# Cross-attention and ternary FFN on one core: A's scale from norms, prologue work spread over eight steps, row maxima in PSUM, a new block order, and the FFN two steps earlier

## The reference

```python
h = layernorm(x)                                   # (16, 128, 256)
q = rmsnorm(heads(h @ Wq)) * gq                    # over each head's 128
k = rmsnorm(heads(ctx @ Wk)) * gk
v = heads(ctx @ Wv)
x = x + concat(softmax(q @ k.T / sqrt(128)) @ v) @ Wo
h = layernorm(x)
# bit_linear: activations rounded to 8 bits per row, weights to -1, 0, 1 by their mean |w|
h = silu(bit_linear(h, w_gate)) * bit_linear(h, w_up)
x = x + bit_linear(rms_norm(h) * ln_weight, w_down)
```

## Time and profile before

| | before |
|---|---|
| median of 3 runs | 529.06 us |
| profiled execution: time, span | 530.74 us, 528.90 us |
| mean granted TensorE clock | 0.974 of full |
| busy share TensorE, VectorE, ScalarE, GpSimd | 80%, 92%, 81%, 73% |
| first 27.2 us | loads, maxima, scales |
| 27.2 to 107.9 us | steps 0 to 7 |
| 107.9 to 413.8 us | 56 steps |
| 413.8 to 442.1 us | attention's tail, first FFN steps |
| from 442.1 us | FFN |

### The profile page before, as it was taken

The page is one execution under the profiler, slowest core; times in us unless marked ns, Lnnn a source line. Parts: engine busy times, 40 slices in busy tenths (PEclk is TensorE's granted clock), DMA queues, the critical chain, the costliest instruction groups (busy, mean ns, idle before and its releaser), DMA issues.

```text
span 528.9 us, 14416 instructions
## 1 busy us (share of the span) xinstructions
PE 420.7 (80%) x4456; PEld 316.9 (60%) x4456; DVE 484.6 (92%) x1303; ACT 428.1 (81%) x1447; POOL 386.8 (73%) x312
## 2 busy tenths in 40 slices
PE   0248275699999999999999999999999556678885
PEld 0137264577777777677776777777777343345554
DVE  1989969899999999999999999999999857899995
ACT  1079488498988989889898898988989638799983
POOL 1015628479989899998989999899989943666772
PEclk9999877799999999999999999999999999899999
DMA  7950713154734445354444535445464530000001
GB/s 278 347 170 22 233 46 81 41 81 85 155 79 100 99 91 108 79 114 85 99 99 84 114 79 111 87 95 104 89 114 85 117 60 2 1 20 32 30 30 51
DMA packets 145324, 50.16 MB, mean 95 GB/s; under 512 B 135952, under 2 KB 143120, under 8 KB 144784
## 3 DMA queue, kind: packets, MB, share of 16 engines
q1 hardware_dynamic: 144192, 46.68, 39.7%
q10 hardware_dynamic: 1104, 3.15, 1.7%
HBM read 14.16 MB, written 2.10 MB: 31 GB/s over the span
## 4 chain that ended last, share of the span: by engine, by line
DVE 48%; issue 29%; POOL 11%; PE 5%; DMA 3%; ACT 3%; DVEq 1%; POOLq 0%; ACTq 0%
DVE khl L855 9%; DVE khl L837 5%; DVE qhl L812 3%; POOL work L476 3%; DVE smax L808 3%; POOL qshl L482 3%; POOL rkq L497 3%; DVE ham L914 2%; DVE nbias L820 2%; DVE ohl L830 2%; DVE work L979 2%; DMA xs<-in_x 2%; DVE phl L843 2%; DVE kqe L848 1%; PE KQ L1128 1%
## 5 line engine op out<-in xcount | busy, mean ns | idle before, releaser
L576 ACT ACTIVATE work<-SO,nbias,rkq 128x128 f32<-128x128 f32 x256 | 115.1, 479 | 23.9 <-DVE nbias L820 23.8
L351 PE MATMUL KQ<-hT,wqs 128*128 (+1 forms) x1536 | 104.3, 226 | 19.3 <-DVE qhl L812 7.2
L497 POOL TENSOR_TENSOR rkq<-kqe,negh 128x8 f32<-128x8 f32 x65 | 108.6, 1670 | 13.6 <-DVE kqe L848 13.6
L351 PEld LDWEIGHTS KQ<-hT,wqs 128*128 128x128 f16 x1536 | 95.0, 101 | 28.5 <-DVE qhl L812 11.0
L488 POOL TENSOR_TENSOR phl<-work,phl 128x512 f16<-128x512 f32 x64 | 74.1, 1158 | 45.3 <-DVE phl L843 45.3
L351 PE MATMUL EB<-As,ohl 128*128 128x256 f16 x768 | 94.3, 273 | 0.0
L351 PEld LDWEIGHTS EB<-As,ohl 128*128 128x128 f16 x768 | 75.0, 98 | 21.5 <-issue 0.2
L476 POOL TENSOR_TENSOR work<-work,rinv 128x512 f32<-128x512 f32 x64 | 70.0, 1094 | 7.2 <-DVE rinv L789 7.2
L482 POOL TENSOR_TENSOR qshl<-work,qshl 128x512 f16<-128x512 f32 x64 | 75.2, 1174 | 0.1
L351 PE MATMUL SO<-pT,cs 128*128 128x512 f16 x192 | 53.0, 386 | 11.5 <-DMA pT<-phl 10.5
L351 PE MATMUL SO<-kT,qhl 128*128 128x128 f16 x768 | 54.7, 222 | 9.0 <-ACT work L576 6.6
(11 more groups left out here) (159 smaller groups left out, 945.0 us busy)
## 6 DMA issues: line engine op xcount, KB each, us to landing
xs<-in_x SPq DMA_DIRECT2D x4, 512.0 KB, 10.6
wvo<-in_wo SPq DMA_DIRECT2D x1, 2048.0 KB, 18.9
out<-wqs SPq DMA_DIRECT2D x16, 128.0 KB, 1.7
raw<-in_ctxT ACTq DMA_DIRECT2D x1, 1024.0 KB, 5.5
stage<-in_wk SPq DMA_DIRECT2D x1, 1024.0 KB, 13.4
stage<-in_wq SPq DMA_DIRECT2D x1, 1024.0 KB, 16.3
stage<-in_wq ACTq DMA_DIRECT2D x1, 1024.0 KB, 12.7
kT<-khl SPq DMA_TRANSPOSE x64, 2.9
```

The source lines that it names most:

```text
L351: last = matmul(out, lhsT=left(i), rhs=right(j), start=start and n == 0, stop=stop and n == 2)
L497: pool.tensor_tensor(rkq[:, g % 4, :], kqe[:, g % 2, :], negh[:, 0:2 * HG], ALU.pow).then_inc(root_ok, 1)
L576: ins = act.activation(pe[:, s, c], SB[:, c], ACT.Exp, scale=rkq[:, (g - AT_X + 1) % 4, HG + h:HG + h + 1], bias=nbias[:, s, h:h + 1], acc ...
```

## The change

- **A's scale** is no longer from A's maximum. ScalarE sums the squares of Wo (before the splits) and of Wv (end of step 0); a ones matmul adds them over partitions, GpSimd takes both to the power -1/2, and the scale is 2^15 over the product of the two norms. A's high and low parts are written straight from PSUM, two heads at a time, in steps 2 to 5.
- **The scales of the context and Wk** come from ScalarE's sums of absolute values (by 2^-3) in place of VectorE's maxima. Wq keeps its maximum.
- **Spread work.** Statistics, roots, layernorm, transposes, context copies and splits are dealt over steps 0 to 7; x parts 1 to 3 are loaded after Wo and the context; Wq's first group is split first; the absolute sums of the FFN weights move to ScalarE.
- **PSUM.** From step 8 on smax is written to a free PSUM strip, and pss and the key half of kqe read a constant from it as second tensor.
- **Order.** The blocks of a step stand in a new order on all four engines.
- **FFN.** It begins at step 66, with the up projection in TM and the transposes in SO.

```diff
-O_SHIFT = 2.0 ** -12
+O_SHIFT = 2.0 ** -15
+TOP_A = 2.0 ** 15
+SUM_SHIFT = 2.0 ** -3
-FFN_AT = NT + AT_O - AT_GU
+FFN_AT = NT + AT_X - AT_GU
-A_AT = {1: (0, 4), 2: (4, 8)}
-LN_AT = {"start": (0, 2), 0: (2, 4), 3: (4, 6), 4: (6, 7), 5: (7, 8)}
+A_AT = {2: (0, 2), 3: (2, 4), 4: (4, 6), 5: (6, 8)}
+TOT_AT = 1
+STAT_AT = {0: (1, 2), 1: (2, 3), 2: (3, 4)}
+ROOT_AT = {1: (1, 2), 3: (2, 4)}
+APPLY_AT = {2: (4, 6), 3: (6, 8), 4: (8, 10), 5: (10, 12), 6: (12, 16)}
+LN_AT = {"start": (0, 2), 2: (2, 3), 3: (3, 4), 4: (4, 5), 5: (5, 6), 6: (6, 8)}
+C_AT = {2: (0, 1), 3: (1, 2), 4: (2, 3), 5: (3, 4)}
+ABS_AT = {5: 0, 6: 1, 7: 2}
...
+        c_psum = TPf[:, 16:16 + 2 * HG].rearrange("p (s h) -> p s h", s=2)
+        smax_ps = TPf[:, 0:2 * HG].rearrange("p (s h) -> p s h", s=2)
+        def smax_of(b, s):
+            return smax_sb[:, s, :] if isinstance(b, int) and b < 2 else smax_ps[:, s, :]
...
+        splits = [q_split(0), (c_cols(0), cT_f[:, group_cols(0)], 1), k_split(0)]
...
+            for i, (s, src) in enumerate(((cT_in, cT_f), (wk_in, wk_f))):
+                act.wait_ge(s, 16)
+                act.wait_ge(asum_ok, i)
+                act.activation(junk0, src, ACT.Abs, scale=SUM_SHIFT, accum_out=amax[:, i + 1:i + 2]).then_inc(asum_ok, 1)
             ln_high("start")
+            act.wait_ge(wvo_in[0], 16)
+            act.activation(As[:, 0, :, :], wo_f, ACT.Square, accum_out=ssA[:, 1:2]).then_inc(sumA_ok, 1)
             act.wait_ge(scales_ok, 1)
...
-                    act.copy(A_f[:, 2 * i:2 * i + 2, :],
-                             A_banks[i % 4].rearrange("p (h n) -> p h n", h=2)).then_inc(A_cp, 1)
+                    act.wait_ge(Ascl_ok, 1)
+                    copy_scaled(As[:, 0, 2 * i:2 * i + 2, :], A_banks[i % 2].rearrange("p (h n) -> p h n", h=2),
+                                sclA[:, 0:1]).then_inc(A_hi, 1)
+            def A_squares():
+                act.wait_ge(wvo_in[1], 16)
+                act.activation(As[:, 1, 0:H // 2, :], wvT_f.rearrange("p h c -> p (h c)"), ACT.Square,
+                               accum_out=ssA[:, 0:1]).then_inc(sumA_ok, 1)
...
-                    dve.tensor_scalar(pss[:, s, :], psm[:, s, :], 1.0 / P_SCALE, None, ALU.mult).then_inc(pss_ok, 1)
+                        dve.tensor_tensor(pss[:, s, :], psm[:, s, :], c_psum[:, 0, :], ALU.mult).then_inc(pss_ok, 1)
...
-                    dve.tensor_reduce(smax[:, s, :], heads(SB), axis=AX_X, op=ALU.max).then_inc(smax_ok, 1)
+                    dve.tensor_reduce(smax_of(b, s), heads(SB), axis=AX_X, op=ALU.max).then_inc(smax_ok, 1)
...
+                        dve.scalar_tensor_tensor(out=kqe[:, s, 0:HG], in0=kss[:, s, :], scalar=epsk[:, 0:1],
+                                                 in1=c_psum[:, 1, :], op0=ALU.add, op1=ALU.mult).then_inc(kse_ok, 1)
...
+                if now(b, g) == TOT_AT:
+                    dve.wait_ge(totA_ps, 1)
+                    dve.tensor_scalar(nrmA[:, :], MB[:, 4:6], TINY ** 2, None, ALU.max).then_inc(totA_ok, 1)
+                    dve.wait_ge(nrmA_ok, 1)
+                    link(dve.tensor_scalar(sclA[:, :], nrmA[:, 0:1], nrmA[:, 1:2], TOP_A, ALU.mult, ALU.mult))
...
-                    for s in (klo_ok, qlo_ok, exp_ok, olo_ok):
+                    for s in (klo_ok, qlo_ok, qse_ok, nb_ok):
                         te.wait_ge(s, NT)
...
-                    for banks, w in ((KQ, wgq), (SO, wuq)):
+                    for banks, w in ((KQ, wgq), (TM, wuq)):
```

More of the change, by code:

```diff
@@ L162, in build_program @@
         c_in = sem("c_in")
[L163 removed]
+        wvo_in = [sem(f"wvo_in{i}") for i in range(2)]
         g_in = sem("g_in")
@@ L308, in steps @@
             straight(step, G * (2 + F_CHUNKS), FFN_AT)
[L309 to L312, removed]
+            for s in range(2 * G):
+                if FFN_AT + s < NT + AT_E + 1:
+                    step((FFN_AT + s) // G, (FFN_AT + s) % G)
+                ffn(s // G, s % G)
             with eng.Fori(2, B // G) as b:
@@ L498, in step @@
                                        ALU.pow).then_inc(root_ok, 1)
[L499 to L504, removed]
+                for i in range(*C_AT.get(now(b, g), (0, 0))):
+                    c_low(i)
+                if live(b, g, AT_X):
+                    s = (g - AT_X) % 2
+                    need(pool, phi_ok, b, g, AT_X)
+                    need_dma(pool, pT_in[s], b, g, AT_X, 2)
+                    pool.tensor_tensor(phl[:, s, 1, :], pn[:, s, :], phl[:, s, 0, :],
+                                       ALU.subtract).then_inc(plo_ok, 1)
             def ffn(b, g):
@@ L588, in step @@
                     copy_scaled(qhl[:, g, 0, :], QB, gcol[:, 0:1]).then_inc(qhi_ok, 1)
[L589 to L600, removed]
+                A_out(now(b, g))
                 if live(b, g, 0):
@@ L785, in step @@
                                       ALU.add, ALU.mult).then_inc(qse_ok, 1)
+                for i in range(*STAT_AT.get(now(b, g), (0, 0))):
+                    statistics(i)
+                if (g - AT_E - 1) % G == G - 1 and live(b, g, AT_E + 1):
+                    bb = batch(b, g, AT_E + 1)
+                    dve.wait_ge(x1_ok, bb + 1)
+                    dve.bn_stats(st6[:, bb, :], xs[:, bb, :]).then_inc(f_st, 1)
                 if live(b, g, AT_X):
@@ L1016, in step @@
             def step(b, g):
+                if live(b, g, AT_SSQ):
+                    s = (g - AT_SSQ) % 2
+                    need(te, qslo_ok, b, g, AT_SSQ)
+                    need(te, qse_ok, b, g, AT_SSQ, 1)
+                    if now(b, g) == TOT_AT + 1:
+                        te.wait_ge(totA_ok, 1)
+                    if not isinstance(b, int) and g == 0:
+                        te.wait_ge(wscl_ok, 1)
+                    for h in range(HG):
+                        for a in range(2):
+                            ins = te.matmul(MB[:, h:h + 1], lhsT=qshl[:, s, a, h * P:(h + 1) * P],
+                                            rhs=ones[:, 0:1], start=a == 0, stop=a == 1)
+                    ins.then_inc(ssq_ps, 1)
                 if live(b, g, 0):
-                    if now(b, g) in range(G):
-                        te.wait_ge(w_lo, 3 + 2 * g)
+                    if now(b, g) == 0:
+                        te.wait_ge(w_lo, 1)
+                    if now(b, g) in range(1, G):
+                        te.wait_ge(w_lo, 2 + 2 * g)
                     if now(b, g) == 2 * G - 1:
                         te.wait_ge(w_lo, CT_SPLIT)
-                        te.wait_ge(hlo_ok, B // 2)
                     tok = bass.ds(b * SKV, SKV)
```

384 lines of the change are left out of this document (188 added, 196 removed).

## The result

The changed kernel takes 510.10 us (median of 4 runs, 508.54 to 513.24), the kernel before on the same chip 529.59: ratio 0.9635, 95% interval 0.9579 to 0.9690. Faster, as forecast, but by 19.5 us and not by 39, and outside the range of 478 to 507.

What follows compares the result with a forecast made beforehand. VectorE, busy without a gap but partly held by GpSimd, was taken to bound the loop. Loop -14, start -19 and tail -6 gave -39 from 530.74, 491.7, less 1.68 for the median: 490 us, range 478 to 507.

Steps and rivals of the forecast that it cites:

- (c): Start: maxima become ScalarE sums; Wo landing near 21, its squares eat 0.8, step 0's queries at 27.5, not 31.06.
- (b): Loop, new block order: 5.22 a step against 5.461, and 5.0 against 5.35 in eight steps behind it; together -14.
- (g): Tail: FFN enters two steps sooner, first matmuls near 433 instead of 439.04; -6, bounds -2 and -9.
- (a): Loop, port: PSUM operands free nbias, pss and kqe from holds, at +0.05 each for reading; VectorE 4.90 a step.
- R3: Rival, loop: holds remain, on the reciprocal (first form) or on nbias despite its PSUM operand; 508; chance 0.08.
- R4: Rival, loop: the kT chain becomes the bound, 6.15 a step, slower at 543; chance 0.05.
- (d): Steps 0 to 3: a layernorm and A's reductions and maximum exchange go; pow 3 at 55.5 instead of 62.76 (-7.3).
- (f): Steps 5 to 7: FFN reductions leave VectorE, ScalarE bounds; pow 7 at 89, including 2 for misses, instead of 107.93.
- (e): Step 3 to 4: the wait chain on A's maximum and scale goes; pow 4 at 62.3 instead of 79.52.
- R5: Rival, start: it gives half, loaded ScalarE brings pow 7 only to 98; 499; chance 0.09.

Runs made afterwards that it cites:

- after: The profiled execution of the changed kernel, compared with the kernel before: 513.24 us, the longest of four runs; median 510.10, ratio 0.9635.
- the filled kernel: Changed kernel with Wo's squares later, A's clamp early, kT's load first, FFN root later and fnm early, plus useless matmuls in TensorE's pauses: 494.64 us, ratio 0.9307.
- the kernel with the later root: Changed kernel with GpSimd's first FFN root moved from ahead of pow 64 to behind phl's subtraction of step 65: 506.03 us, ratio 0.9538.
- all edits: Changed kernel with Wo's squares later, A's clamp early, kT's load first, FFN root later and fnm early: 497.07 us; variants add the sums' matmul (496.08) or filling (494.64).

## Why the prediction missed, point by point

Three steps failed: Wo's landing in (c), the 5.0 a step behind the loop in (b), and the path of the tail in (g), where two FFN operations came to stand ahead of attention's last ones. Besides, the sum had no term for TensorE's clock.

- **(a) the port: near in sum, wrong in its parts.** I freed nbias, pss and kqe alike and valued nbias' 0.32. In the new order nbias isn't held even in SBUF (150), and pss, which I hadn't priced, would be (856). The PSUM operand's +0.05 each was 0. R3's first form, a held reciprocal, is refuted (165), and with it my reading of the rule in (a); that its 508 lay near the result is luck.
- **(b) the block order: right for the loop.** Forecast 5.22; 5.259 in after, and 5.22 to 5.26 in all other profiles with pss in PSUM. That is 1.8 of the miss. For the eight steps behind it I forecast 5.0 from the engines' sums; 5.42 came (3.4 of the miss), 5.115 with kT first, so 2.4 of it went with kT's place behind pT, though some profiles without that edit show 5.21. In (b) I had this chain down as 9.7 in 10.4 with 0.7 to spare: at 5.0 a step 0.3 is spare, and R4, dismissed as a whole, holds in part for just these steps.
- **(c) the start: the step that failed first.** "From a landing near 21": the 18.9 of the row of before plus its issue. That row showed Wo and Wv on one semaphore, and 18.9 was put down to the wrong one: the same view of before lists 25.3 for Wv, and with a semaphore each it is 18.9 for Wv, half as large, and 24.6 for Wo. I had written "which eats 0.8"; it ate 5.6 more. Pow 3 came 5.7 late. There moving the squares is worth 1.5 and leaving them out 2.9, since moved they stand ahead of step 0's work. The norm's exchange with GpSimd I had priced by its work (1.6), not as a wait of TensorE's queue.
- **(d) to (f): the list held, the clock didn't.** From pow 3 to 7 I forecast 33.5; after took 35.5, the filled kernel 32.7. At full clock (the kernel with the later root) it is 32.4, so the list with its 2 us for misses was even 1.1 high; TensorE at half speed then costs 3.1, and by pow 8 4.5. I had no term for it, though before shows such clocks too (0.71 from 64 to 80, 0.78 from 80 to 98). In (e) the sum gives 62.5, not 62.3.
- **(g) the tail: wrong in sign, and the largest miss.** Forecast -6, measured +2.5. I moved the FFN two steps forward and didn't follow what else moved. In the new order of GpSimd's step the FFN root comes ahead of the pow, where before it came behind; it waits 1.69, runs 2.59, and pow 64, phl, kT and the last scores queue behind: 4.3. And ScalarE's first FFN activation is now ahead of the last exp and waits for an fnm that VectorE has last: 3.0. What I had named as late next, the Silu with its table load, was not: in the kernel with the later root the table is loaded at 412.91 and the Silu waits for its matmul until 414.75.
- The sign of the whole was right, and so was the order start, loop, tail (-11.2, -8.8, +2.5 for -19, -14, -6). The rivals covered the start (R5) and the loop singly; what came was a half miss in each of three stages, and no rival, nor the range up to 507, had that.

Open: why single kT landings take up to 4.7 instead of 2.9; 2 us of pow 3 (57.5 against 55.5 at best, with all edits); 1 to 2 of the tail; and what sets the clock's level in one execution and not in the next.

## What to carry to other kernels

When instructions are reordered in a step that also has exceptional cases (first, last, preparation), follow each exceptional instruction to its new neighbours: here one root ahead of a pow, instead of behind, cost 4.3 us of a tail that was to give 6. A held operation is worth what waits behind it, not its length, and freeing it pays only if the next operation isn't held in turn: test port edits and order together. And where two transfers share a semaphore, a profile can put down the landing of the first to the other: 18.9 for Wo, whose own was 24.6.

## What the runs showed of the hardware

- A 128x4 tensor_scalar between SBUF tiles took 856 ns in the mean, each ending with GpSimd's 128x512 subtraction, a 128x4 reciprocal in the changed kernel's loop, mostly inside the same subtraction, 165, and the same scaling as a tensor_tensor with a PSUM second operand 153.
- TensorE's granted clock in the same instructions of the same code was 0.5 in one profile and 1.00 in another; useless matmuls in its pauses kept it at 1.00 from 50 to 98 us, and the kernel was 0.4% to 0.6% faster.
